# First layer of a two-layer kernel: ScalarE sums the squares of a normalization by head, with eight accumulating squares of 64 columns

## What is computed

```python
def step(carry, inp):                     # one chunk of 64 tokens
    W, bb = carry
    xq_c, xk_c, xv_c = inp
    Z1 = xk_c @ W + bb
    mu = Z1.mean(-1, keepdims=True)
    std = jnp.sqrt(Z1.var(-1, keepdims=True) + EPS)
    x_hat = (Z1 - mu) / std               # over the 64 values of a head
    y = g * x_hat + be
    gxh = (y - (xv_c - xk_c)) * g
    grad_x = (HD * gxh - gxh.sum(-1, keepdims=True)
              - x_hat * (gxh * x_hat).sum(-1, keepdims=True)) / (HD * std)
    Wn = W - einsum(eta * xk_c, grad_x)
    bn = bb - (eta * grad_x).sum(-2, keepdims=True)
    Zq = xq_c @ Wn + bn
    out = xq_c + g * ((Zq - mu2) / std2) + be    # mu2, std2: those of Zq
```

## Time and profile before

| what | us |
|---|---|
| median of 3 runs | 946.85 (946.74 to 947.41) |
| the profiled execution | 945.96 |
| its span, first to last instruction | 944.2 |
| PE busy | 888.2 (94%) |
| DVE busy | 770.7 (82%) |
| POOL busy | 635.6 (67%) |
| ACT busy | 554.7 (59%) |
| mean granted TensorE clock | 0.974 of full speed |

### The profile page before, as it was taken

One profiled execution on the slowest core, in us unless ns is written; L12 is line 12 of the kernel. 1 busy time (PEld: TensorE's weight loads), 2 busy tenths in 40 slices (PEclk: granted clock), 3 DMA queues, 4 the chain that ended last, 5 costly groups with the idle time before them and its releaser, 6 DMA issues.

```text
span 944.2 us, 19724 instructions
## 1 busy us (share of the span) xinstructions
PE 888.2 (94%) x7768; PEld 612.3 (65%) x7768; DVE 770.7 (82%) x1180; ACT 554.7 (59%) x833; POOL 635.6 (67%) x579
## 2 busy tenths in 40 slices
PE   2898999999998899999999999999999999999997
PEld 2666787877776688655665666666665665665564
DVE  7779898899886637788888888888888888879876
ACT  4554566666664363665766655756656666666662
POOL 4567788888884050956955966955966965866872
PEclk9598999999999899899999999999999999999999
DMA  8100000000000500110210220110120110120110
GB/s 220 42 2 2 2 2 3 2 2 3 2 2 2 154 26 23 57 57 10 66 49 25 71 75 8 60 57 24 65 77 10 57 64 20 61 77 20 45 51 24
DMA packets 24964, 38.27 MB, mean 41 GB/s; under 512 B 9316, under 2 KB 15480, under 8 KB 22824
## 3 DMA queue, kind: packets, MB, share of 16 engines
q1 hardware_dynamic: 23240, 34.74, 12.1%
q10 hardware_dynamic: 1632, 2.27, 0.8%
HBM read 28.29 MB, written 1.43 MB: 31 GB/s over the span
## 4 chain that ended last, share of the span: by engine, by line
PE 60%; DVE 22%; issue 11%; POOL 3%; ACT 3%; DMA 1%; SPq 0%; POOLq 0%; DVEq 0%
PE bank L1162 12%; PE bank L1164 10%; PE bank L1163 10%; DVE hdh L957 6%; PE bank L1319 3%; PE bank L1435 3%; PE quad L1467 3%; PE quad L1211 3%; DVE add L966 3%; DVE mx L950 2%; PE quad L1202 2%; PE quad L1370 2%; PE bank L1276 2%; PE bank L1486 1%; PE quad L1291 1%
## 5 line engine op out<-in xcount | busy, mean ns | idle before, releaser
L950 DVE TENSOR_REDUCE mx<-quad 128x4 f32<-128x2048 f32 x64 | 146.3, 2286 | 38.5 <-PE quad L1467 38.4
L1130 POOL CAST hdh<-xn 128x512 fp32r<-128x512 f32 x96 | 65.7, 684 | 155.3 <-ACT xn L627 155.3
L644 ACT ACTIVATE ex<-quad 128x2048 f32<-128x2048 f32 x64 | 120.6, 1884 | 58.8 <-PE quad L1477 58.8
L1132 POOL TENSOR_TENSOR hdl<-hd,hdh 128x512 fp32r<-128x512 f32 x96 | 129.6, 1350 | 7.7
L1132 POOL TENSOR_TENSOR hdl<-xn,hdh 128x512 fp32r<-128x512 f32 x96 | 128.8, 1342 | 7.7
L1162 PE MATMUL bank<-hdh,W2h 128*128 128x512 f32 x256 | 113.5, 443 | 5.7 <-DVE hdl L960 4.7
L627 ACT ACTIVATE xn<-bank,b1c 128x512 f32<-128x512 f32 x128 | 87.8, 686 | 28.5 <-POOL hdl L1132 19.7
L627 ACT ACTIVATE hd<-bank,b1c 128x512 f32<-128x512 f32 x112 | 76.9, 687 | 43.8 <-PE bank L1164 26.9
L1163 PE MATMUL bank<-hdh,W2l 128*128 128x512 f32 x256 | 101.1, 395 | 0.0
L1164 PE MATMUL bank<-hdl,W2h 128*128 128x512 f32 x256 | 101.0, 395 | 0.0
L1162 PE MATMUL bank<-cH,W1h 128*128 128x512 f32 x192 | 80.9, 422 | 0.7 <-DVE cL L977 0.7
(11 more groups left out here) (303 smaller groups left out, 2188.7 us busy)
## 6 DMA issues: line engine op xcount, KB each, us to landing
cwB<-gate_rows SPq DMA_DIRECT2D x16, 1024.0 KB, 4.6
kx<-kqh SPq DMA_DIRECT2D x32, 64.0 KB, 2.1
qx<-kqh SPq DMA_DIRECT2D x32, 64.0 KB, 2.1
W1r<-in_L_ffn_W SPq DMA_DIRECT2D x1, 1024.0 KB, 10.7
kx<-kql SPq DMA_DIRECT2D x16, 64.0 KB, 2.1
qx<-kql SPq DMA_DIRECT2D x16, 64.0 KB, 2.1
rec<-rec_rows SPq DMA_DIRECT2D x32, 32.0 KB, 2.1
out<-fin SPq DMA_DIRECT2D x4, 256.0 KB, 2.3
```

The source lines that it names most:

```text
L644: act.activation(ex[:, t % 2, :, :], quad[:, :, :], ACT.Exp, scale=float(AD) ** -0.5).then_inc(ROUND["exps_ready"], 1)
L950: dve.tensor_reduce(mx[:, t, :, 0], quad[:, :, :], AX_X, ALU.max, negate=True).then_inc(ROUND["score_max"], 1)
L1130: pool.tensor_copy(hdh[:, m % RING, :], tile(n)).then_inc(ROUND["pool_split"], 1)
L1132: pool.tensor_tensor(hdl[:, m % RING, :], tile(n), hdh[:, m % RING, :], ALU.subtract).then_inc(ROUND["pool_split"], 1)
```

## The change

`squares(s)` becomes eight Square activations, one per head, each over 64 columns, each with `accum_out`, so that ScalarE writes the head's sum of squares to `sm` itself. The last one signals `z_sumsq`. `sum_squares` is removed from VectorE's list, and the semaphore `z_squared` is gone. The query half (`squares_q`, `sum_squares_q`) is as before.

```diff
                     if s >= 4:
                         act.wait_ge(CHUNK["zq_ready"], s - 3)
-                    act.activation(by_pair(sqz[:, :]), z_of, ACT.Square).then_inc(CHUNK["z_squared"], 1)
+                    for h in range(8):
+                        last = act.activation(sqz[:, 64 * h:64 * h + 64], z_of[:, h // 2, h % 2, :], ACT.Square, accum_out=sm[:, s % 4, 0, h:h + 1])
+                    last.then_inc(CHUNK["z_sumsq"], 1)
...
-            def sum_squares(s):
-                if s in LIVE:
-                    dve.wait_ge(CHUNK["z_squared"], s + 1)
-                    dve.tensor_reduce(sm[:, s % 4, 0, :], g3(sqz[:, :]), AX_X, ALU.add).then_inc(CHUNK["z_sumsq"], 1)
-
...
-                centre(s - 1), sum_squares(s), sum_squares_q(s), rdev(s), xhat(s)
+                centre(s - 1), sum_squares_q(s), rdev(s), xhat(s)
```

More of the change, by code:

```diff
@@ L278, in build @@
         N_CHUNKS = ("tokens_high", "tokens_low", "keys_ready", "keys_taken", "queries_ready", "queries_taken", "xk_ready", "xk_taken", "u_ready", "u_taken",
-            "z_ready", "z_squared", "z_sumsq", "z_dev", "z_rdev", "xhat_ready", "scaled_ready", "gx_ready", "gx_sum", "gx_centred", "rate_ready",
+            "z_ready", "z_sumsq", "z_dev", "z_rdev", "xhat_ready", "scaled_ready", "gx_ready", "gx_sum", "gx_centred", "rate_ready",
             "gx_xhat", "gx_xhat_sum", "xhat_part", "grad_less", "grad_ready", "bias_ready", "dw_ready", "bias_high", "bias_split", "state_updated",
```

## The result

The changed kernel takes 952.39 us, median of 5 runs (950.83 to 953.32), against 947.41 (946.74 to 949.59) before: ratio 1.005, 95% interval 1.0034 to 1.0066. It is slower, by 5 us where 15 were forecast; 952.39 lies just inside the range of 952 to 978. The profiled execution took 952.39, its span is 950.5 us.

A forecast was written before the change was run, and what follows sets the result against it. The order of waits in the engines' lists, not throughput of the removed reduction, was taken to bound the kernel. Loop 8.3, step 30 1.2, first ten steps 0.7 and clock 5 sum to +15 on 946.85: 962 us, range 952 to 978.

The forecast's parts named there:

- The clock: In the loop, TensorE's idle time (stand) in A drops the clock to 1.2 GHz (fall) once a period: +5 us.
- Rival 2: No clock falls: the forecast sum without its +5, 957 us; chance 0.15.
- The first ten steps: Steps before the loop: late `take_u` in steps 0 and 2 against VectorE's relief, net +0.7 us, bounds -1 and +4.
- The relief of VectorE: Steps 4, 6 and 7, where VectorE is bound: the removed reduction gives back some 0.9 us in all.
- The price of a pair: On ScalarE, a 64-column square plus its accumulator read, overlapping its follower: 0.22 us, 1.76 us for eight.
- rival 1: The accumulator read is not overlapped, 0.31 us a pair: 973 us; chance 0.18.
- A: Loop step with s mod 4 = 2: late `take_u` makes TensorE wait for the key features, +1.16 us a period.
- B: Loop step after A: the later deviation, with 0.15 us of slack before the bias rows, costs +0.49 us a period.
- C and D: Last two steps of a loop period, where TensorE has `att`, which covers the delay: 0.
- Step 30: After the five periods: hands over no keys, but `normed` stands directly before the bias rows: +1.2 us.
- Rival 3: Cheap pairs of 0.18 us: loop 5, step 30 +0.8, early steps 0, no falls, 952.5 us; chance 0.10.
- Rival 4: VectorE's relief wins: eight passages (five periods, steps 4, 7, 30) gain 0.6 each, -5, 942 us; chance 0.06.

The follow-up runs named there:

- experiment 3: Changed kernel with `take_u` issued after five of the eight pairs, the other three and the query half's square behind it: 960.42 us, ratio 1.014.
- experiment 4: Changed kernel with the query half's square first, then three pairs, `take_u`, five pairs: 957.76 us, ratio 1.0118.
- experiment 5: Kernel before with its one square replaced by eight pairs writing to spare columns, VectorE's reduction kept: 954.02 us, ratio 1.0083.
- experiment 11: Changed kernel with two copies of 1024 columns on ScalarE ahead of the loop, which runs about 1.4 us later: 954.88 us, ratio 1.0089.
- experiment 1: The kernel before, profiled once more without an edit: one run of 948.30 us.
- experiment 6: Changed kernel with one square in place of the pairs and no sum, the deviation reading a constant; VectorE's reduction stays removed: 944.32 us, ratio 0.9979.
- experiment 7: Eight pairs in steps 4 to 8 only, the one square and VectorE's reduction in all other steps: 944.38 us, ratio 0.9982 to the kernel before.

## Why the prediction was wrong

- **The clock: the step that failed.** I took one fall a period, +5 us. There was none in any of the ten periods of the two profiles of the changed kernel, none in the five periods each of experiments 3, 4, 5 and 11, none in five with stands of 1.5 us, and one in five with stands of 2.0. I had taken the two falls as the consequence of stands, although the stand of 1.04 without one lay beside them and the same stand of 0.69 us can go either way (experiment 1). Rival 2 was this term's other side: no falls in the loop. Its own 957 us was still too high, by what follows. The Trainium skill, TensorE: Matmul & The Clock Gate, Part 1, has the clock drop after an idle window; its forecast, no falls for stands of 1 us, held for the loop, while the fall behind 0.69 us in the kernel before is not explained by it.
- **The first ten steps**, +0.7 forecast with bounds of -1 and +4, -2.3 to -2.9 measured: outside the bounds. The late `take_u` in steps 0 and 2 was right: 6.39 to 7.06 and 9.20 to 9.73, +1.2 where I had +1.6. The relief of VectorE was mis-sized: 0.9 against 1.5 to 2.5 (experiment 6), because I gave step 4 far less than the whole 0.6 of a reduction; steps 4 and 7 even gained 0.85 in one pair of profiles, for which I have no reason. The clock, which I had not counted here, gave the changed kernel 0.8 in step 4 (experiment 7) and, against the first profile alone, another 1.2 in steps 7 and 8. The rest is step 1, which moves by some tenths between profiles of one kernel (10.44 and 9.95 before).
- **The price of a pair**, 0.22 taken, 0.20 measured; eight take 1.59 us, not 1.76. The overlap of the read with its follower was the right choice; rival 1 is out. The 0.24 by the Trainium skill, ScalarE: Activation LUTs, section on what ACT_TABLE_LOAD costs, is above the measured 0.20 too.
- **The loop.** A +1.03 (forecast 1.16), B +0.25 (0.49), C and D 0 (0): +1.29 a period and 6.5 in five, against 8.3. With the measured 1.59 us my own arithmetic gives A 0.99 and B 0.32. The place of the stand in A, that in B, and the cover of C and D came as described. The sum was right not to take the 0.15 us off B, though I called it slack: it was none. What I had as one gate in A is three: `take_u`, the query half's square through VectorE's list, and the deviation through GpSimd to B's bias product; I named the last two only as shifting along. Step 30: +1.0 (1.2).
- **Rival 3**, cheap pairs, has 952.5 us, the measured time, and that is luck: its pairs of 0.18 us were not there, its loop and step 30 (+5.8) are below the measured 7.5, and its 0 for the first ten steps is above the measured -2.3 to -2.9. That 952.39 fell into the stated range rests on the same cancelling.
- **Rival 4**, the relief wins: wrong in the loop (experiment 6, period 30.66), right in part in steps 4 and 7, where its 1.5 to 2.5 us stand against 7.5.

The sum again with what was measured: 6.5 + 1.0 - 2.3 to -2.9 + 0 = +4.6 to +5.2, against 5.0 between the medians. Of the ten microseconds by which I was off, the falls in the loop are 5, the first ten steps 3 to 3.6, the pairs 2.

## What to carry to other kernels

A removed instruction on the chain of waits is worth nothing if the bound engine comes to the same place no earlier; a kernel with the removal alone (experiment 6) tells that in one run. Ask of each moved microsecond which steps it lands in: these pairs are free in C and D, a gain in steps 4 to 8, and the whole loss in A and B, so the version to keep has them in steps 4 to 8 only (0.2% under the kernel before, just clear of the noise). Before freeing one gate, list everything queued behind the same late instruction, or the next gate takes its place.

## What the runs showed of the hardware that I had not expected

- A square of 64 columns with its accumulator read costs ScalarE 0.20 us from start to start, the two halves 0.09 to 0.12 each, and reads overlap activations on both sides. In a row of pairs the recorded durations creep up (0.22 to 0.27 us and 0.19 to 0.25 within one step), while the starts stay 0.20 apart.
- A ScalarE instruction that waits for a sum just read by ScalarE itself starts 0.3 us behind the read when nothing stands between (191.67 and 191.97 in experiment 4, and 0.26 to 0.31 in all 16 even steps there), against 0.1 for a neighbour that does not wait for the sum.
- The same stand of TensorE gave a fall of the clock in one execution and none in another: 0.69 us in two executions of one kernel (experiment 1), two stands of 1.4 us in step 4 of two kernels (experiment 7). Of five equal stands of 2.0 us in one execution one was followed by a fall. With the loop 1.4 us later a fall came behind a stand that had none before (experiment 11). What decides was not settled here.
